# Attention scores as 24-row tiles of the array with one head per 32 rows; maxima split on GpSimd, second LayerNorm scaled on ScalarE

## The chip, the cores and the metric

The kernel runs on one core of one Trainium2 chip. The metric is the device time of an execution in microseconds (us). Engines: PE is TensorE, PEld its weight loads, DVE is VectorE, ACT is ScalarE, POOL is GpSimd, SP is SyncE, which here only issues transfers. The engines run on their own and wait for each other through semaphores.

## The reference, cut to what matters

The input is 32 sequences of 128 tokens with 128 channels (4096 tokens). Layer 0 is a modulated linear map with a clip and a mixture of 8 experts, 2 for each token. Layer 1 is an adapter, attention with 16 heads of 8 channels inside each sequence, and a second mixture of experts. The change touches this part:

```python
h = _layernorm(x, ln1_g, ln1_b)                      # 128 channels
q, k, v = jnp.split(h @ w_qkv + b_qkv, 3, axis=-1)   # each to (sequence, 128 tokens, 16 heads, 8)
scores = jnp.einsum('bqhd,bkhd->bhqk', q, k) / np.sqrt(8)
attn = jax.nn.softmax(scores, axis=-1)
o = jnp.einsum('bhqk,bkhd->bqhd', attn, v).reshape(B, S, D)
x = x + o @ w_o + b_o
h = _layernorm(x, ln2_g, ln2_b)                      # then gate, top 2 of 8, experts, weighted sum
```

## The kernel before, in words

The program is a chain of stages, each a block with its own instruction list for every engine, and a barrier between two: `setup` and `layer0`, `experts0`, `pre_attention`, `attention`, `experts1`, `finish`. In the profiled execution `pre_attention` runs from about 264 to 363 us, `attention` from 363 to about 650 us with its tail.

**pre_attention** goes over eight groups of four sequences. It blends the expert rows, runs the adapter and the first LayerNorm, and computes q and k transposed (channels on partitions, 512 tokens wide). Each is stored in two parts, a high one rounded to fp32r (`high_part`, ACT, L1078) and the rest (`lows`, DVE, L1030), so that products of parts keep fp32's precision. SP writes a group's four arrays to DRAM in one transfer (`store`, L961), and behind it on SP's queue stand the fetches for group n + 3 (L955, L860).

**attention** goes over 32 sequences s, in rounds; u = s mod 4. SP loads q and k for two sequences at a time: `load_pair` puts three parts one above the other on 96 partitions (q high, low, high; k high, high, low), so one matmul adds three products of parts. Four heads lie together on 32 rows, and a head is picked by masks: km holds k four times with all heads but one zeroed (`mask_k`, one of the four on POOL, L1426, three on ACT, L1553), qm holds the same for q, filled by 12 small transfers for each pair (L1410). Thus one matmul gives the scores of four heads as 128x512:

```python
nc.tensor.matmul(ps1[:, g % 2, :], qp[b][:, g, tok(u)], km[p][:, g]...)            # score, L1589
nc.tensor.matmul(ps2[:, g % 2, :]..., kp[b][:, g, tok(u)], qm[b][:, g, :, tok(u)]) # shift, L1596
nc.tensor.matmul(ps2[:, g % 2, :], selr[:, g, :], mxT[p][:])                       # shift, L1598
```

The order on PE is written out by hand. A round for s has four steps g = 0 to 3: the score of sequence s + 1 into one of two banks of ps1, then the shift of s into one of two banks of ps2. The shift computes the scores again, transposed (keys on partitions), and adds the negated maxima, which come transposed as mxT. Then follow: the output projection of s - 3 (L1634), `mix` of s - 1 (probabilities times values, L1616), `turn_max` (transposes of the maxima of s + 1, L1605), and `total` of s - 1 (sums, L1625). `mix` and `total` use four column tiles of 32.

DVE takes maxima over ps1 (L1473), four for each sequence; score g waits for maximum g - 2, since it uses the same bank. Then DVE splits the maxima into a high part and a rest (L1480, L1482), which `turn_max` waits for. It also divides (L1487, L1490) and adds the projection (L1495). ACT takes four exponentials of ps2 (L1565), masks k, and copies the transposed maxima (`copy_max`, L1545); the next round's first shift waits for this copy. POOL masks k, spreads the values into a block diagonal (`spread_v`, L1435), and sends rows.

Second LayerNorm and routing of a group of four sequences run inside the rounds, two groups behind, at fixed u: DVE takes variances in u = 3, POOL the reciprocal root in u = 1 (L1257), DVE normalises in u = 0 (L1272), PE transposes in u = 1 (L1281), computes gate logits in u = 2 (L1298) and ranks in u = 3 (L367). POOL scatters rows to DRAM with indirect transfers (L404), three in u = 1 and five in u = 2, and joins the streams (L1264). After the last round the same steps run for the last two groups one after another, with 8 scatters each.

## Time and profile before

| | us |
|---|---|
| median of 3 timed runs | 926.86 (926.55 to 927.62) |
| span of the profiled execution, first to last instruction | 835.4 |
| difference, around the span | 91.5 |
| PE busy in the span | 614.0 |
| DVE busy | 531.2 |
| ACT busy | 349.9 |
| POOL busy | 427.8 |

The profiled execution's own time isn't given beside its span; the median of the timed runs stands for it. The span is that of one execution, from the first instruction to the last. Busy time is the sum over an engine's instructions; where matmuls overlap they count once. A row of the timeline has a start, a duration, the engine, the line, the tile written and those read, their shapes and a count; in brackets stands the idle time before it and what ended it. A count over 1 means that a run of the same instructions was merged, and the duration is that of the whole run. An fp32 matmul leaves two records, an fp32r matmul one.

### The profile page before, as it was taken

How to read it: one execution, taken by the hardware profiler on the slowest of the kernel's cores; microseconds unless marked ns; L12 is line 12 of the kernel's file. 1: busy time of each engine (PE TensorE's matmuls, PEld its weight loads, DVE VectorE, ACT ScalarE, POOL GpSimd, SP SyncE). 2: the span in 40 equal slices, each digit the busy share in tenths (PEclk: the TensorE clock that was granted, in tenths of full speed). 3: DMA queues.
4: the chain of work that ended last, by engine and by line, in shares of the span. 5: the costliest groups of instructions: out<-in, count | busy, mean ns of one | idle time of the engine just before them, and what ended most of it. 6: DMA issues, size and time to landing. Idle time of an engine off the chain costs nothing. (4 is left out here: it accounts for less than half of the span.)

```text
span 835.4 us, 19142 instructions
## 1 busy us (share of the span) xinstructions
PE 614.0 (73%) x5686; PEld 501.2 (60%) x5686; DVE 531.2 (64%) x1601; ACT 349.9 (42%) x673; POOL 427.8 (51%) x528
## 2 busy tenths in 40 slices
PE   1799932999990675629999988999740599999920
PEld 0466622989980443416777666667530499999910
DVE  1455542767761789854788688789543377777708
ACT  0433411555440232326777676767410244334300
POOL 1177760767765454361444675676573055555530
PEclk9999985999995599966999999999955699999975
DMA  7711153777753254733444344356115788888318
GB/s 233 150 52 52 51 98 96 222 200 206 212 154 84 58 164 154 207 101 61 90 97 105 93 100 105 77 127 124 29 42 76 252 273 248 245 247 250 104 61 266
DMA packets 98617, 116.28 MB, mean 139 GB/s; under 512 B 16225, under 2 KB 78209, under 8 KB 98433
## 3 DMA queue, kind: packets, MB, share of 16 engines
q1 hardware_dynamic: 78784, 92.38, 41.9%
q0 software_dynamic: 9216, 18.96, 7.2%
q10 hardware_dynamic: 10560, 4.24, 2.5%
q8 instruction: 29, 0.48, 0.2%
q14 instruction: 28, 0.22, 0.1%
HBM read 81.84 MB, written 33.69 MB: 138 GB/s over the span
## 5 line engine op out<-in xcount | busy, mean ns | idle before, releaser
L404 POOL DMA_INDIRECT dispatch_rows<-row,index x128 | 128.2, 1002 | 96.2 <-DVE index L385 61.1
L740 POOL DMA_INDIRECT expert_rows<-fo,to x80 | 78.4, 980 | 84.8 <-DVE fo L1773 70.3
L1473 DVE TENSOR_REDUCE mneg<-ps 128x4 f32<-128x512 f32 x128 | 86.8, 690 | 41.7 <-PE ps L1589 39.5
L740 POOL DMA_INDIRECT expert_rows<-eo,to x80 | 77.1, 964 | 56.2 <-ACT eo L831 31.1
L1565 ACT ACTIVATE prob<-ps 128x512 f32<-128x512 f32 x128 | 76.3, 598 | 53.4 <-PE ps L1598 48.0
L713 DVE CAST xh<-psT 128x256 fp32r<-128x256 f32 x80 | 34.0, 425 | 97.1 <-PE psT L683 97.1
L1763 PE MATMUL psO<-wb,fh 128*128 128x128 f32 x640 | 77.8, 275 | 0.0
L731 PE MATMUL psA<-xh,wh 128*128 128x256 f32 (+1 forms) x240 | 75.4, 314 | 0.0
L1589 PE MATMUL ps<-km,qp 96*128 96x512 f32 x128 | 58.5, 460 | 23.0 <-POOL km L1426 17.4
L1763 PEld LDWEIGHTS psO<-wb,fh 128*128 128x128 f32 x640 | 74.9, 192 | 0.0
L731 PE MATMUL psA<-xh,wl 128*128 128x256 f32 (+1 forms) x240 | 68.7, 286 | 0.0
L731 PE MATMUL psA<-xl,wh 128*128 128x256 f32 (+1 forms) x240 | 68.4, 285 | 0.0
L1809 ACT ACTIVATE fh<-psA,wb 128x256 f32<-128x256 f32 x80 | 33.6, 471 | 80.2 <-PE psA L731 80.2
L1426 POOL TENSOR_SCALAR km<-kp,const 96x512 fp32r<-96x512 f32 x32 | 52.6, 1644 | 23.7 <-DMA kp<-qk_parts 18.8
L1553 ACT ACTIVATE km<-kp,const 96x512 fp32r<-96x512 f32 x96 | 61.9, 711 | 6.8 <-PEq L950 5.5
L1596 PE MATMUL ps<-qm,kp 96*128 96x512 f32 x128 | 55.4, 433 | 0.7 <-ACT mxT L1545 0.4
L1598 PE MATMUL ps<-mxT,selr 128*128 128x512 f32 x128 | 53.2, 416 | 0.0
L1589 PEld LDWEIGHTS ps<-km,qp 96*128 96x128 f32 x128 | 25.8, 203 | 41.1 <-issue 25.9
L731 PEld LDWEIGHTS psA<-xh,wh 128*128 128x128 f32 (+1 forms) x240 | 44.1, 184 | 0.0
L731 PEld LDWEIGHTS psA<-xl,wh 128*128 128x128 f32 (+1 forms) x240 | 44.0, 183 | 0.0
L1435 POOL COPY vb<-V 128x32 f32 (+1 forms) x128 | 21.1, 209 | 44.4 <-PE psAO L1625 44.4
L731 PEld LDWEIGHTS psA<-xh,wl 128*128 128x128 f32 (+1 forms) x240 | 43.7, 182 | 0.0
(203 smaller groups left out, 1504.1 us busy)
## 6 DMA issues: line engine op xcount, KB each, us to landing
wb<-in_W1b SPq DMA_DIRECT2D x40, 578.0 KB
w<-in_W SPq DMA_DIRECT2D x40, 304.0 KB
qk_parts<-qk SPq DMA_DIRECT2D x8, 1024.0 KB, 4.9
qp<-qk_parts SPq DMA_DIRECT2D x48, 128.0 KB, 3.1
kp<-qk_parts SPq DMA_DIRECT2D x48, 128.0 KB, 3.7
qm<-qk_parts SPq DMA_DIRECT2D x192, 32.0 KB
xs<-dispatch_rows SPq DMA_DIRECT2D x40, 129.0 KB
xt<-dispatch_rows SPq DMA_DIRECT2D x40, 129.0 KB
```

The lines of the kernel that those rows point to most:

```text
L404: pool.indirect_dma_start(out=m.xbuf, out_offset=bass.IndirectOffsetOnAxis(ap=r.index[b][:, c:c + 1], axis=0), in_=r.row[b][:, c // TOPK, ...
L713: v.tensor_copy(z.xh[q][:], z.psT[:, q, 0:SLOTS]).then_inc(z.x_high, 1)
L731: ins = z.m.nc.tensor.matmul(out, w[k][q][:, columns], x[k][q][:], start=(k == 0), stop=(k == 2), skip_group_check=True)
L740: pool.indirect_dma_start(out=m.ybuf, out_offset=bass.IndirectOffsetOnAxis(ap=to[b][:, a:a + 1], axis=0), in_=out[b][:, a, :], in_offset=N ...
L1426: ins = nc.gpsimd.tensor_scalar(km[p][:, :, j, :], kp[b][:, :, tok(u)].bitcast(F32), mask(j), None, ALU.mult)
L1473: ins = nc.vector.tensor_reduce(mneg[p][:, g, :], ps1[:, g % 2, :].rearrange("p (j k) -> p j k", j=4), AX_X, ALU.max, negate=True)
L1553: ins = nc.scalar.activation(km[p][:, :, j, :], kp[b][:, :, tok(u)].bitcast(F32), ACT.Copy, scale=mask(j))
L1565: nc.scalar.activation(prob[p][:, g, :], ps2[:, g % 2, :], ACT.Exp, scale=ATT_SCALE).then_inc(exped, 1)
L1589: nc.tensor.matmul(ps1[:, g % 2, :], qp[b][:, g, tok(u)], km[p][:, g].rearrange("p j k -> p (j k)"), start=True, stop=True).then_inc(score ...
L1596: nc.tensor.matmul(ps2[:, g % 2, :].rearrange("p (j k) -> p j k", j=4), kp[b][:, g, tok(u)], qm[b][:, g, :, tok(u)], start=True, stop=False)
L1598: nc.tensor.matmul(ps2[:, g % 2, :], selr[:, g, :], mxT[p][:], start=False, stop=True).then_inc(shifted, 1)
L1763: ins = nc.tensor.matmul(psO[:, q, a * P:(a + 1) * P], h[q][:, k, a * P:(a + 1) * P], wb[b][:, WIDE + k * P:WIDE + (k + 1) * P], start=(k ...
```

## The change

q and k are laid out anew: head 4g + j has 32 rows of partitions (32g to 32g + 31) and its own place j in the free dimension; 24 of the rows are used, three parts of 8 channels. The weights of q and k are reordered once on ACT so that the projection gives this order. Three arrays each of q and k are stored now (the doubled high part is written by ACT with one activation of twice the width), in four transfers a group, and a pair is loaded in eight transfers. Masks, km and qm are gone. A score is now four matmuls with 24 rows and 128 columns, on rows 32g and up; the shift of group (g + 2) mod 4 stands between them, on other rows. Splitting the maxima moves to POOL (`part_max`). Normalising moves from DVE to ACT, with an offset (minus mean times root) from DVE. The root moves from u = 1 to u = 0, and scatters are spread as 3, 3 and 2 over u = 0, 1 and 2.

```diff
+    m.wqk, m.qkb = m.sb("wqk", [P, 2 * P]), m.sb("qkb", [P, 2])
...
-def load_pair(m, sp, n, b):
-
-    for side, parts in ((m.qp[b], (0, 1, 0)), (m.kp[b], (2, 2, 3))):
-        for r, a in enumerate(parts):
-            sp.dma_start(side[32 * r:32 * r + 32].bitcast(F32),
-                         m.qk_dram[a, :, bass.ds(n * PAIR, PAIR)].rearrange("(g r) t -> r g t", g=HG)
-                         ).then_inc(m.pair_in[b], 16)
+def load_pair(m, sp, i, b):
+
+    half = slice(b * PAIR, (b + 1) * PAIR)
+    for g in range(HG):
+        for side, at in ((m.qp[b], 0), (m.kp[b], SPLIT)):
+            source = m.qk_dram[bass.ds(i, 1), g, at:at + SPLIT, :, half].rearrange(
+                "a s (d j) t -> (a s d) j t", j=HG)
+            sp.dma_start(side[32 * g:32 * g + HROWS].bitcast(F32), source).then_inc(m.pair_in[b], 16)
+
+
+PAIR_LOADS = 16 * 2 * HG
...
+                    for g in range(HG):
+                        sp.dma_start(m.qk_dram[bass.ds(n, 1), g].rearrange("a c p t -> (a p) c t"),
+                                     qk[b][32 * g:32 * g + 32].bitcast(F32)).then_inc(qk_out[b], 16)
...
+                    both = qk[b][:, 0:3:2, :] if w == 0 else qk[b][:, 3:5, :]
+                    nc.scalar.activation(both, bc(psQK[:, w, :].unsqueeze(1), P, 2, GW), ACT.Identity,
+                                         bias=m.qkb[:, w:w + 1]).then_inc(high, 1)
+
+                act.wait_ge(m.late_ld, LATE_LOADS)
+                nc.scalar.activation(m.wqk[:].rearrange("p (g d j) -> p g d j", d=DK, j=HG),
+                                     m.wqkv[:, 0:2 * P].rearrange("p (g j d) -> p g d j", j=HG, d=DK),
+                                     ACT.Copy).then_inc(ordered, 1)
...
-def post_normalise(q, dve, n):
+def post_centre(q, dve, n):
 
     dve.wait_ge(q.rooted, n + 1)
-    wait(dve, q.turned, n)
+    wait(dve, q.normed, n)
+    q.m.nc.vector.scalar_tensor_tensor(out=q.offset[:], in0=q.mv[:, :, 0], scalar=-1.0, in1=q.rstd[:],
+                                       op0=ALU.mult, op1=ALU.mult).then_inc(q.centred, 1)
+
+
+def post_normalise(q, act, n):
+
+    act.wait_ge(q.centred, n + 1)
+    wait(act, q.turned, n)
     for t in range(GT):
-        ins = q.m.nc.vector.tensor_scalar(q.norm[:, t, :], post_stream(q, n, t), q.mv[:, t, 0:1],
-                                             q.rstd[:, t:t + 1], ALU.subtract, ALU.mult)
+        ins = q.m.nc.scalar.activation(q.norm[:, t, :], post_stream(q, n, t), ACT.Identity,
+                                       bias=q.offset[:, t:t + 1], scale=q.rstd[:, t:t + 1])
     ins.then_inc(q.normed, 1)
...
-                    hold(m, sp, shifted, 8 * (n - 1))
-                    hold(m, sp, km_pool, 2 * (n - 1))
-                    hold(m, sp, km_act, 2 * (n - 1))
                     if not isinstance(n, int):
-                        load_pair(m, sp, n, b)
-                    if isinstance(n, int):
-                        sp.wait_ge(zeroed[b], 1)
-                    for j in range(4):
-                        for r, a in enumerate((0, 1, 0)):
-                            rows = slice(32 * r + 8 * j, 32 * r + 8 * j + 8)
-                            source = m.qk_dram[a, :, bass.ds(n * PAIR, PAIR)].rearrange("(g j r) t -> j r g t", g=HG, j=4)[j]
-                            sp.dma_start(qm[b][rows, :, j, :].bitcast(F32), source).then_inc(qm_in[b], 16)
+                        hold(m, sp, shifted, 8 * (n - 1))
+                        load_pair(m, sp, i, b)
                 table_sync(tiles, sp)
 
             @block.gpsimd
...
-                def mask_k(s, u, i):
-                    p, b = u % 2, u // 2
-                    if p == 0:
-                        pool.wait_ge(pair_in[b], 96 * (i + 1))
-                    hold(m, pool, scored, 4 * (s - 1))
-                    for j in range(KM_POOL):
-                        ins = nc.gpsimd.tensor_scalar(km[p][:, :, j, :], kp[b][:, :, tok(u)].bitcast(F32), mask(j), None,
-                                                      ALU.mult)
-                    ins.then_inc(km_pool, 1)
+
+                def part_max(s, p):
+                    pool.wait_ge(maxed, 4 * s + 4)
+                    hold(m, pool, turned, s - 1)
+                    x = xm[p][:]
+                    hi, lo = (bass.AP(x.tensor, x.offset + w, [list(x.ap[0]), [32, HG], [P, 4]]) for w in range(2))
+                    nc.gpsimd.tensor_copy(hi.bitcast(F32R), mneg[p][:]).then_inc(link, 1)
+                    hold(m, pool, link, s + 1)
+                    nc.gpsimd.tensor_tensor(lo, mneg[p][:], hi, ALU.subtract).then_inc(parted, 1)
 
...
-                parts = {1: range(0, 3), 2: range(3, 8)}
-                for s, u, i in rounds(pool, SEQS, GT, head=3 * GT):
-                    mask_k(s, u, i)
+                part_max(0, 0)
+                parts = {0: range(0, 3), 1: range(3, 6), 2: range(6, 8)}
+                for s, u, i in rounds(pool, SEQS, GT, head=3 * GT, tail=GT):
+                    if not is_last(s, SEQS):
+                        part_max(s + 1, (u + 1) % 2)
+                    if u == 0 and due(i - 2):
+                        post_root(post, pool, i - 2)
+                    spread_v(s, u % 2)
                     if u in parts and due(i - 3):
                         post_scatter(post, pool, i - 3, 0, parts[u])
-                    if u == 1 and due(i - 2):
-                        post_root(post, pool, i - 2)
-                    if not first(s):
-                        spread_v(s - 1, (u - 1) % 2)
-                    if is_last(s, 2):
-                        nc.gpsimd.memset(qm[1][:].bitcast(F32), 0.0).then_inc(zeroed[1], 1)
                     if u == 3 and due(i - 2):
                         post_join(post, pool, i - 2)
-                spread_v(SEQS - 1, 1)
...
+                    wait(dve, parted, s - 1)
...
-                    dve.wait_ge(maxed, 4 * s + 4)
-                    wait(dve, turned, s - 1)
-                    x = xm[p][:]
-                    hi, lo = (bass.AP(x.tensor, x.offset + w, [list(x.ap[0]), [32, 4], [130, 4]]) for w in range(2))
-                    nc.vector.tensor_copy(hi.bitcast(F32R), mneg[p][:]).then_inc(link, 1)
-                    dve.wait_ge(link, s + 1)
-                    nc.vector.tensor_tensor(lo, mneg[p][:], hi, ALU.subtract).then_inc(parted, 1)
...
+                    if u == 0 and due(i - 2):
+                        post_normalise(post, act, i - 2)
...
-                def score(s, u, i, g):
-
-                    p, b = u % 2, u // 2
-                    wait(pe, maxed, 4 * s + g - 1)
-                    nc.tensor.matmul(ps1[:, g % 2, :], qp[b][:, g, tok(u)], km[p][:, g].rearrange("p j k -> p (j k)"),
-                                     start=True, stop=True).then_inc(scored, 1)
-
-                def shift(s, u, g):
-
-                    p, b = u % 2, u // 2
-                    wait(pe, exped, 4 * s + g - 1)
-                    nc.tensor.matmul(ps2[:, g % 2, :].rearrange("p (j k) -> p j k", j=4), kp[b][:, g, tok(u)], qm[b][:, g, :, tok(u)],
-                                     start=True, stop=False)
-                    nc.tensor.matmul(ps2[:, g % 2, :], selr[:, g, :], mxT[p][:], start=False, stop=True
-                                     ).then_inc(shifted, 1)
+                def score(s, u, g, j):
+
+                    head = slice(32 * g, 32 * g + HROWS)
+                    return nc.tensor.matmul(ps1[:, g % 2, j * P:(j + 1) * P], qp[u // 2][head, j, tok(u)],
+                                            kp[u // 2][head, j, tok(u)], start=True, stop=True, skip_group_check=True)
+
+                def shift(s, u, g, bank, j):
+
+                    head = slice(32 * g, 32 * g + HROWS)
+                    return nc.tensor.matmul(ps2[:, bank, j * P:(j + 1) * P], kp[u // 2][head, j, tok(u)],
+                                            qp[u // 2][head, j, tok(u)], start=False, stop=(j == 3),
+                                            skip_group_check=True)
+
+                def lower(s, u, g, bank):
+
+                    rows = slice(32 * g, 32 * g + 32)
+                    nc.tensor.matmul(ps2[:, bank, :], selr[rows, :], mxT[u % 2][rows, :], start=True, stop=False,
+                                     skip_group_check=True)
 
...
                     for g in range(HG):
                         if more:
-                            score(*nxt, g)
+                            wait(pe, maxed, 4 * (s + 1) + g - 1)
                         if g == 0:
-                            if u % 2 == 0:
-                                pe.wait_ge(qm_in[u // 2], 16 * 12 * (i + 1))
                             pe.wait_ge(mxT_done, s + 1)
-                        shift(s, u, g)
+                        wait(pe, exped, 4 * s + g - 1)
+                        if more:
+                            score(s + 1, nxt[1], g, 0)
+                        lower(s, u, opposite(g), g % 2)
+                        for j in range(4):
+                            if more and j < 3:
+                                ins = score(s + 1, nxt[1], g, j + 1)
+                                if j == 2:
+                                    ins.then_inc(scored, 1)
+                            ins = shift(s, u, opposite(g), g % 2, j)
+                        ins.then_inc(shifted, 1)
                     if u == 1 and due(i - 2):
                         post_turn(post, pe, i - 2)
```

## Rows read from the trace of the kernel before

**Rows 1.** The page, part 1: busy time, share of the span, instructions of each engine.

```profile
PE 614.0 (73%) x5686; PEld 501.2 (60%) x5686; DVE 531.2 (64%) x1601; ACT 349.9 (42%) x673; POOL 427.8 (51%) x528
```

**Rows 2.** Stretches of attention: us, busy time by engine (count), PEclk, DMA share, GB/s.

```profile
377.00:390.00 13.00, 11.24 (x27) 8.11 (x27) 5.50 (x10) 7.79 (x13) 1.56 (x1) 0.50 0.13 20
...
430.00:590.00 160.00, 146.58 (x1944) 109.89 (x1942) 128.10 (x379) 114.88 (x199) 102.44 (x166) 0.99 0.46 103
```

**Rows 3.** Timeline of DVE: maxima of seven of the sequences.

```profile
400.05 2.95 DVE L1473 TENSOR_REDUCE mneg<-ps 128x4 f32<-128x512 f32 x4 [1.90 <-PE ps L1589]
...
429.82 2.79 DVE L1473 TENSOR_REDUCE mneg<-ps 128x4 f32<-128x512 f32 x4
...
509.81 2.67 DVE L1473 TENSOR_REDUCE mneg<-ps 128x4 f32<-128x512 f32 x4
...
517.67 2.67 DVE L1473 TENSOR_REDUCE mneg<-ps 128x4 f32<-128x512 f32 x4 [0.33 <-PE ps L1589]
...
524.17 2.66 DVE L1473 TENSOR_REDUCE mneg<-ps 128x4 f32<-128x512 f32 x4
...
531.11 2.81 DVE L1473 TENSOR_REDUCE mneg<-ps 128x4 f32<-128x512 f32 x4 [2.46 <-PE ps L1589]
...
538.66 2.68 DVE L1473 TENSOR_REDUCE mneg<-ps 128x4 f32<-128x512 f32 x4
```

**Rows 4.** Timeline of PE, one head group: start, us, engine, line, tiles, count.

```profile
511.36 0.39 PE L1589 MATMUL ps<-km,qp 96*128 96x512 f32 x1
511.59 0.40 PE L1596 MATMUL ps<-qm,kp 96*128 96x512 f32 x1
```

**Rows 5.** Timeline of PE, 519.6 to 523.3 us: the rest of a round.

```profile
520.23 1.08 PE L1616 MATMUL psAO<-prob,vb 128*32 128x128 f32 x32
521.61 0.66 PE L1605 MATMUL psM<-const,xmx 128*128 128x128 f32 x4 [0.30 <-DVE xmx L1482]
...
523.21 0.50 PE L1589 MATMUL ps<-km,qp 96*128 96x512 f32 x1
```

**Rows 6.** Waits of 377 to 600 us: waiting <- releaser: total us, times, longest.

```profile
PE ps L1589 <- POOL km L1426: 5.9, 5, 1.8
```

**Rows 7.** Timeline of PE elsewhere: 128 columns in fp32, 256 in fp32r.

```profile
300.91 1.06 PE L1117 MATMUL psD<-x1T,wd 128*32 128x128 f32 x8
...
721.80 0.28 PE L731 MATMUL psA<-xh,wl 128*128 128x256 f32 x1
721.92 0.28 PE L731 MATMUL psA<-xh,wh 128*128 128x256 f32 x1
```

**Rows 8.** Groups by line, POOL, 377 to 600 us: busy us, mean ns | idle before.

```profile
L404 POOL DMA_INDIRECT dispatch_rows<-row,index x41 | 40.7, 994 | 32.3 <-DVE index L385 22.2 <-issue 8.2 <-PE ps L1589 1.2
L1435 POOL COPY vb<-V 128x32 f32 (+1 forms) x120 | 19.8, 209 | 44.4 <-PE psAO L1625 44.4
L1257 POOL TENSOR_TENSOR rstd<-var,minus_half 128x4 f32<-128x4 f32 x6 | 6.4, 1060 | 4.5 <-DVE var L1250 4.4
```

**Rows 9.** Timeline: four 128x128 with scale and bias on ACT, four normalised on DVE.

```profile
35.20 1.50 ACT L590 ACTIVATE y<-psY,vec,dcoef 128x128 f32<-128x128 f32 x4
...
604.09 1.28 DVE L1272 TENSOR_SCALAR norm<-X,mv,rstd 128x128 f32<-128x128 f32 x4 [2.20 <-POOL rstd L1257]
```

**Rows 10.** Timeline, start of the attention stage.

```profile
369.00 1.19 PE L1589 MATMUL ps<-km,qp 96*128 96x512 f32 x2 [11.50 <-POOL km L1426]
...
376.42 0.60 ACT L1545 ACTIVATE mxT<-psM 128x512 fp32r<-128x512 f32 x1 [9.82 <-PE psM L1605]
...
377.16 0.77 PE L1596 MATMUL ps<-qm,kp 96*128 96x512 f32 x1 [0.35 <-ACT mxT L1545]
```

**Rows 11.** The page, part 6: DMA issues, KB each, median us to landing.

```profile
qk_parts<-qk SPq DMA_DIRECT2D x8, 1024.0 KB, 4.9
```

**Rows 12.** Timeline of SPq, a store and what follows it.

```profile
297.19 0.39 SPq L961 DMA_DIRECT2D qk_parts<-qk  x1
...
298.17 1.02 SPq L860 DMA_DIRECT2D gr<-expert_rows  x1
```

110 lines of the change are left out of this document (50 added, 60 removed).

## The prediction, made before the changed kernel was timed

> **What bounds the kernel now.** I read the page's busy shares first. Over the whole span TensorE leads with 73% and VectorE has 64% [rows 1], but that mixes all stages and decides nothing. All edits sit in attention and in the stage ahead of it, so the second view is the table of stretches. Between 430 and 590 us TensorE is busy for 146.6 of 160 us at full clock, VectorE for 128.1, ScalarE for 114.9, GpSimd for 102.4 [rows 2]: TensorE is the engine to follow there, and VectorE is close behind. Third, the maxima on the timeline of VectorE, four reductions for each sequence, mark the rounds. Early rounds, in which no second LayerNorm or routing is due, are (429.82 - 400.05)/5 = 5.95 us long. With that work a set of four (u = 3, 0, 1, 2) takes 7.86 + 6.50 + 6.94 + 7.55 = 28.85 us [rows 3]. The stretch from 430 to 590 holds 22 rounds, 7.2 us each, the same.
>
> Inside a round, four steps (one for a group of four heads) come first. On TensorE a step is three matmuls of 512 columns, 0.23 us apart [rows 4], so 0.69 us; VectorE's four reductions take 2.67 us, 0.67 each [rows 3]. So the steps are paced by two engines at once, and a faster TensorE alone gains next to nothing in them. The rest, from the mixing matmuls to the next score, takes 523.21 - 520.23 = 2.98 us, of which 0.30 is a wait for the split maxima: 2.7 us of work [rows 5]. What isn't work in the rounds is mostly a wait for the masked keys: 5.9 us in 5 waits for GpSimd [rows 6], and the 2.46 us for which VectorE stands at 531.11 [rows 3] are its echo.
>
> **The step after the change.** Three loads and three matmuls become nine of each: four scores and four shifts of 24 rows by 128 columns, and one 32-row matmul of 512 columns. Scores use one row group, the other five the opposite one. No row shows an array split by rows. The nearest rows: 32 records of matmuls into four column tiles (L1616) take 1.08 us [rows 5], 8 records of the same 128 fp32 columns without tiles (L1117) take 1.06 [rows 7]. So four tiles really run side by side, loads included. For loads of 128 columns, the fp32r pairs at L731 stand 0.12 us apart [rows 7], so a load costs 0.12 at most. For matmuls: 512 fp32r columns cost 0.23, 256 cost 0.12; I take 0.06 for 128. If the two row groups run side by side and a load hides behind its own group's matmuls, the longer side is the 512 columns, the first shift, and three more shifts paced by loads: 0.23 + 0.06 + 3 x 0.12 = 0.65 us. That is below VectorE's 0.67, so VectorE paces the steps.
>
> A plain round, from its first score at 0: the last score lies behind three loads, reduction 0 starts at 0.7 (three loads 0.36, one matmul 0.06, about 0.17 until a result is out, that is 0.39 of record less 0.23 of spacing in rows 4, and the handover), reductions end at 1.37, 2.04, 2.71 and 3.38. Step 3 waits for reduction 1, starts at 2.1 and ends at 2.75; projection 0.3; then 2.7 us: 5.8 us against 5.95.
>
> One rule speaks against the edit. The Trainium skill (TensorE: Matmul & The Clock Gate, section LDWEIGHTS) says that a load costs its columns and not its rows. By it the 24-row loads are no cheaper than the 96-row ones, there are three times as many, and side by side is all that saves the step; the sum above prices them in full already, so it stays.
>
> **Maxima on GpSimd.** Cast and subtraction leave VectorE (about 0.4 us in a round) and become two GpSimd instructions of 128x16. GpSimd's copy of 128x32 takes 0.21 us, its power of 128x4 takes 1.06 [rows 8]. I take 0.21, since these are a copy and a subtraction: with three handovers 0.6 us, so the transposes may start at 3.38 + 0.6 = 4.0. TensorE gets there at 2.75 + 0.3 + 1.0 = 4.05: hidden. At 1.06 each they'd be ready at 5.7 and cost 1.6 us a round, 50 us in 31 rounds; a gain isn't possible beyond VectorE's 0.4. Queued behind them on GpSimd: the root (1.06), the spread values (4 x 0.21 in record, 0.65 in fact) and two or three scatters, each 0.99 plus 0.3 of issue [rows 8]. In a round u = 0 that is 1.06 + 0.65 + 3.9 = 5.6 us, and the next maxima come 5.8 us or more after the last: it fits with little to spare. The masked key (1.6 us a round of GpSimd, 1.9 of ScalarE) is gone, and the 12 small loads for each pair with it.
>
> **Normalise on ScalarE.** It must come in round u = 0 between the exponentials and the copy of the next maxima, which the next round's first score now waits for. The chain: reductions end at 3.4 (as in a plain round), GpSimd splits until 4.0, root until 5.1, VectorE's offset until 5.4, four activations of 128x128 take 1.50 us (the same form at L590) [rows 9] until 6.9, copy of the maxima 0.6 until 7.5. TensorE alone would need 5.8: a new stall of 1.7 us. Round u = 0 goes from 6.50 to 7.5. Round u = 1 is the plain 5.8 and four transposes, 0.5 (between rows 5's 0.66 for four of the same form and their spacing): 6.3 against 6.94. Round u = 2 has four fp32 matmuls of 136 columns, two records each, each record a little over the 0.13 of 128 columns [rows 7], so 1.15: 6.95 against 7.55. In round u = 3 VectorE is last: 7.86 less the 0.4 that moved, and the late start less 0.3: 7.15. Sum 27.9 against 28.85, or 0.95 for four rounds; for 22 rounds -5 us. The five early rounds go from 5.95 to 5.8, -0.8.
>
> **The start.** In attention's first 27 us TensorE has a granted clock of 0.50 [rows 2], the row from 377 to 390, which is 1.2 GHz, after it stood idle. The stage opens at 362.8, but the first score runs at 369.00, having waited 11.5 us, last for GpSimd's masked key, and the first shift at 377.16 [rows 10]. After: scores at once, at half clock 16 loads of 0.24 each (twice the 0.12), 3.8 us, then 0.9 until the last reduction ends, 0.6 for GpSimd, 1.1 for transposes at half clock, 0.6 for the copy: first shift 7.0 us into the stage, at 369.8 instead of 377.2. I take -7. From 377.16 to the maxima at 400.05 there are three rounds in 22.9 us [rows 3, 10]. After: two at half clock with steps of 1.3, 4 x 1.3 + 2.6 = 7.8 each, and one of 5.9: 21.5, -1.4.
>
> **What is added ahead.** The store of q and k grows from 1024 KB, landing in 4.9 us [rows 11], to 1536 KB in four issues of 0.39 each [rows 12]. The last one is waited for by the whole stage: 1.2 us of issues and about 0.4 for ScalarE's doubled write of k: +1.7. The other seven have the fetch at L860 behind them on SP's queue. Its issue stands there for 1.02 us anyway [rows 12], since it waits for its buffer, so 0.8 us of the 1.2 are covered; with more traffic beside it I book +1 in all, 0 to +7 as bounds. ScalarE's doubled writes of groups 0 to 6 lie in its idle time. At the end, twice, normalising takes 1.50 and an offset of 0.2 instead of 1.28 on VectorE [rows 9], and this chain is serial: +1.
>
> **Sum.** -7 - 1.4 - 0.8 - 5 + 1.7 + 1 + 1 = -10.5 us. The profiled execution has a span of 835.4 us; the three timed runs have a median of 926.86, so 91.5 us lie around the span, and nothing in them changes. 926.9 - 10.5 = 916 us. On its own this case ranges from 904 to 926.
>
> **Rivals.**
> 1. Loads don't run side by side. Then nine loads at 0.12 make a step of 1.08 us: step 3 ends at 4.3, not 2.75, +1.55 a round, 31 rounds, less about 2 where VectorE is last in u = 3: +46, so 962 us, slower than before. Against it are the column tiles, whose 32 loads fit into 1.08 us [rows 5]; for it, that none of these is a row tile. It decides from a step of 0.77 us on: 4 x 0.77 - 2.75 = 0.33 us, which in 31 rounds is the whole gain.
> 2. A load waits for its own group's matmul. Step: 0.23 + 4 x (0.12 + 0.06) = 0.95 us, +1.05 a round, +31: 947 us. The unsplit array doesn't do that: its 512-column matmuls stand at 0.23 with a load each [rows 4]. The Trainium skill has this rule (same page, Part 3, The mechanism: a load overlaps a running matmul only when the row group differs); the trace disagrees for the whole array and shows no row tile.
> 3. 128 columns of fp32r cost what fp32 costs. An fp32 matmul of 128 columns is two records, 8 in 1.06 us [rows 7], so 0.22 to 0.26 each. No row has fp32r below 256 columns. Step 0.23 + 4 x 0.22 = 1.11: +1.7 a round, +50: 966; with the row groups one after another too, 1.99 a step, (1.99 - 0.65) x 4 x 31 = 166 and less the same 2 more: 1080.
> 4. GpSimd comes late. If scatters and root don't fit between two maxima, the split waits about 0.6 us in 18 rounds: +11, and the time is 927, no change.
>
> **Chances.** Forecast 0.54, of which 0.02 shows too little to be told from no change; rival 1 0.12, rival 2 0.06, rival 3 0.15, rival 4 0.08; 0.05 for a gain beyond 904, if shorter waits also keep the clock up. Within 0.2% (1.9 us, what a measurement of this kernel can tell) fall the 0.02 and 0.05 of rival 4. Slower: 0.33 and 0.02 of rival 4, 0.35. Faster: 0.58. The range that leaves out under 2 in 10 goes from 900 to 968, over most of rivals 1 to 3.
>
> **What would show it.** In the changed profile: first maxima of a round 0.67 us apart each (a step over 0.8 on TensorE is rival 1, 2 or 3: the spacing of shifts tells which, 0.12 mine, 0.18 the second, 0.22 the third); no wait for a masked key; first shift about 7 us after the stage opens; ScalarE's copy of maxima last in u = 0, rounds of 7.5 us there and 5.8 in the early ones; transposes of maxima that wait for GpSimd under 0.2 us. I am wrong if early rounds are over 5.95 us.

## The result: 8 to 9 per cent slower

Changed kernel 1006.39 us (median of 4, 1001.98 to 1017.28), kernel before 927.24 beside it; ratio 1.083, 95% interval 1.078 to 1.088. The forecast was 916, its range 900 to 968. It was wrong, in sign too.

On the chip of that comparison the kernel before takes 94 us more and the changed one 99 us more than on the chips of most later runs. In the changed kernel's profile there, engines wait for something that the trace can't name, also in stages that the change doesn't touch (waiting <- releaser: us in total, times, longest):

```profile
ACT fh L1814 <- remote: 49.7, 11, 4.7
DVE xh L715 <- remote: 45.1, 15, 3.4
ACT s L607 <- remote: 24.7, 5, 7.7
ACT mxT L1548 <- remote: 24.6, 4, 6.2
```

A later run of the same kernel on another chip (e1_after) has no such wait and takes 907.33 us against 833.58 for the kernel before: ratio 1.090, 1.086 to 1.094. The loss is the same in kind, and traces are compared there: span 900.9 against 834.2 (e0_before). The page of e1_after, busy time and PEclk in 40 slices (compare [rows 1]):

```profile
span 900.9 us, 20237 instructions
PE 650.8 (72%) x6454; PEld 550.9 (61%) x6454; DVE 497.8 (55%) x1509; ACT 310.1 (34%) x610; POOL 383.0 (43%) x559
PEclk9999967999955788658888696867866589999975
```

VectorE, ScalarE and GpSimd have less to do than before, TensorE 38 us more (613.0 in e0_before): its clock is below full in most slices of the attention. Cut into stages (start to end; us; busy time and count by engine; PEclk; DMA share; GB/s), with cuts at the first and last exponential, the kernel before:

```profile
272.00:377.70 105.70, 61.96 (x300) 40.53 (x301) 81.55 (x214) 33.90 (x57) 48.45 (x57) 0.82 0.47 137
377.70:597.90 220.20, 203.88 (x2645) 152.46 (x2648) 167.50 (x478) 158.29 (x273) 117.74 (x201) 0.97 0.43 94
597.90:834.20 236.30, 153.82 (x1384) 150.21 (x1376) 142.67 (x447) 60.57 (x130) 105.35 (x108) 0.81 0.63 183
```

and the changed one:

```profile
272.00:388.80 116.80, 70.77 (x325) 48.27 (x325) 73.01 (x207) 37.31 (x52) 37.10 (x47) 0.72 0.60 154
388.80:665.70 276.90, 233.44 (x3386) 195.42 (x3388) 143.35 (x398) 111.10 (x207) 85.97 (x242) 0.77 0.19 54
665.70:900.90 235.20, 153.55 (x1388) 149.78 (x1380) 140.88 (x442) 63.77 (x137) 105.87 (x108) 0.82 0.63 184
```

Up to 272 us they are alike. The loss is 11.1 us up to the first exponential and 56.7 in the rounds; the tail gains 1.1.

**The start.** SyncE's queue in e1_after, one group (start, us, then line, transfer, count):

```profile
304.81 3.43 SPq L968 DMA_DIRECT2D qk_parts<-qk  x4
308.28 1.54 SPq L961 DMA_DIRECT2D gbu<-cond_rows  x1
309.87 1.82 SPq L862 DMA_DIRECT2D gr<-expert_rows  x1
```

One store issue took 0.39 us before [rows 12]; the four take 3.4, and the fetches behind them are slow too. The last three groups' twelve store issues and the waits between them end at 375.2, and the first score runs at 380.23 (its row and that of the first shift below):

```profile
354.69 20.46 SPq L968 DMA_DIRECT2D qk_parts<-qk  x12
...
380.23 1.12 PE L1580 MATMUL ps<-kp,qp 24*128 24x128 f32 x8 [11.98 <-PEq L956]
387.21 0.79 PE L1593 MATMUL ps<-mxT,selr 32*128 32x512 f32 x1
```

**The rounds.** In round u = 2 of a steady group three engines stand still in turn. TensorE, ScalarE and GpSimd of e1_after:

```profile
573.58 1.08 PE L1611 MATMUL psAO<-prob,vb 128*32 128x128 f32 x32
579.44 0.80 PE L1629 MATMUL psW<-wo,oT 128*128 128x128 f32 x2 [4.78 <-ACT row L395]
...
572.08 1.09 ACT L1556 ACTIVATE prob<-ps 128x512 f32<-128x512 f32 x2 [0.58 <-PE ps L1586]
578.73 0.38 ACT L395 ACTIVATE row<-psW 128x256 f32<-128x256 f32 x1 [5.56 <-DMA dispatch_rows<-row,index]
...
573.35 0.21 POOL L1441 CAST xmx<-mneg 128x16 fp32r<-128x16 f32 x1 [1.10 <-DVE mneg L1486]
573.94 0.65 POOL L1450 COPY vb<-V 128x32 f32 x4
575.11 1.01 POOL L406 DMA_INDIRECT dispatch_rows<-row,index  x1 [0.52 <-issue]
576.43 0.96 POOL L406 DMA_INDIRECT dispatch_rows<-row,index  x1 [0.30 <-issue]
```

Read backwards: TensorE's projection waits for ScalarE's copy of rows (L395), since both use psW. ScalarE may not overwrite its row buffer until the last of the eight scatters of the group before has landed. The last two now stand on GpSimd's queue behind the maxima of the next round and spread_v. Five such rounds take 13.2 to 14.1 us; the same rounds before took 6.7 to 8.7.

The table gives what each run's trace has in the 31 round lengths between first exponentials: their sum, the time in them at a granted clock of 0.50 (1.2 GHz, not 2.4), and, for sequences 12 to 27, the median length by u of the rounds that ran wholly at full clock ("-" where none did). Medians are in us, "before" is the kernel before on the same chip. e8_lower_rows took 897.5 and 898.9 us in two executions and 915.2 and 916.5 in two slow ones, and the table has the middle of the first two.

```
run               median  before  31 rounds  at 0.50  u0    u1    u2     u3
e0_before         832.8   833.6   217.7      15       6.9   7.5   7.2    7.3
e1_after          907.3   833.6   273.5      123      -     6.4   -      -
e2_norm_dve       896.3   833.6   271.1      131      6.3   6.4   -      -
e3b_split_dve     885.3   831.5   258.8      131      -     -     8.2    -
e4_scatter_early  881.5   831.5   252.5      117      -     -     7.2    -
e6_one_store      893.4   831.5   279.9      146      -     6.4   -      -
e7_all_four       857.3   831.5   242.3      101      6.2   6.4   7.2    -
e8_lower_rows     898.2   834.3   281.8      97       7.4   7.8   8.6    -
e9_fill_128       856.3   834.3   244.9      26       7.1   7.5   8.3    8.6
e10_fill_24       861.8   834.3   253.6      104      -     6.7   7.5    -
e11_rows_128      986.2   834.3   378.1      212      -     -     10.0   -
e12_fill_cheap    848.5   833.3   232.9      66       -     6.4   -      7.4
e13_fill_two      846.3   833.3   231.0      61       6.2   6.4   -      7.4
e14_after_fill    937.5   833.3   304.8      96       8.9   7.5   -      8.1
e15b_fill_gaps    841.3   833.3   226.5      42       6.1   6.4   7.7    7.5
e16_fill_three    845.9   832.6   228.1      33       6.5   6.8   7.6    7.9
```

### The profile page after: what moved, and what is told of

Same layout as the page of the kernel before. It is cut to its first block and busy times, and to the rows that moved or that the text cites. A ratio compares the mean times of both kernels' runs of the same rounds, so it can differ in the third digit from the quotient of the medians.

```text
span 1000.2 us, 20237 instructions
## 1 busy us (share of the span) xinstructions
PE 695.5 (70%) x6454; PEld 576.0 (58%) x6454; DVE 490.1 (49%) x1509; ACT 308.2 (31%) x610; POOL 386.0 (39%) x559
## 5 line engine op out<-in xcount | busy, mean ns | idle before, releaser
L1486 DVE TENSOR_REDUCE mneg<-ps 128x4 f32<-128x512 f32 x128 | 82.8, 687 | 116.7 <-PE ps L1580 113.4
L1580 PE MATMUL ps<-kp,qp 24*128 24x128 f32 x512 | 82.2, 328 | 35.9 <-PEq L956 12.7
L1580 PEld LDWEIGHTS ps<-kp,qp 24*128 24x128 f32 x512 | 72.7, 230 | 48.5 <-issue 28.8
L1441 POOL CAST xmx<-mneg 128x16 fp32r<-128x16 f32 x32 | 6.8, 212 | 194.1 <-DVE mneg L1486 194.1
L1586 PEld LDWEIGHTS ps<-qp,kp 24*128 24x128 f32 x512 | 79.4, 235 | 0.2
L1586 PE MATMUL ps<-qp,kp 24*128 24x128 f32 x512 | 75.5, 301 | 0.0
L1593 PE MATMUL ps<-mxT,selr 32*128 32x512 f32 x128 | 68.8, 596 | 0.1
L1611 PE MATMUL psAO<-prob,vb 128*32 128x128 f32 x1024 | 56.4, 388 | 0.6 <-issue 0.6
L1620 PE MATMUL psAO<-prob,const 128*32 128x128 f32 x1024 | 46.3, 319 | 11.1 <-issue 11.1
L809 PE MATMUL psO<-w,eh 88*128 88x128 f32 x320 | 45.8, 290 | 4.5 <-DVE eh L823 4.5
```

The lines of the kernel that those rows point to most:

```text
L809: ins = nc.tensor.matmul(psO[:, q, a * P:(a + 1) * P], h[q][:, k, a * P:(a + 1) * P], w[b][0:HALF, 4 * HALF + k * P:4 * HALF + (k + 1) * P ...
L1486: ins = nc.vector.tensor_reduce(mneg[p][:, g, :], ps1[:, g % 2, :].rearrange("p (j k) -> p j k", j=4), AX_X, ALU.max, negate=True)
L1580: return nc.tensor.matmul(ps1[:, g % 2, j * P:(j + 1) * P], qp[u // 2][head, j, tok(u)], kp[u // 2][head, j, tok(u)], start=True, stop=Tru ...
L1586: return nc.tensor.matmul(ps2[:, bank, j * P:(j + 1) * P], kp[u // 2][head, j, tok(u)], qp[u // 2][head, j, tok(u)], start=False, stop=(j ...
L1593: nc.tensor.matmul(ps2[:, bank, :], selr[rows, :], mxT[u % 2][rows, :], start=True, stop=False, skip_group_check=True)
L1611: nc.tensor.matmul(psO[32 * g:32 * g + 32, p, 0:P], vb[p][:, 4 * g + j, :], prob[p][:, g, j * P:(j + 1) * P], start=(j == 0), stop=(j == 3 ...
```

## The experiments

**e0_before and e1_after**: the two kernels again, three rounds on one chip. 

> The kernel before, unchanged. Theory A (the profile of 835.4 us of span is not an execution like the timed ones, 926.9 us): its span here is about 925 us, and the 91.5 us that I laid around the span lie inside it, as stalls that the first profile doesn't show, in stages that the change doesn't touch too. Theory B (the time around the span is real): span 835, time 927.

> The changed kernel, unchanged. Theory A: time 1002 to 1007 us, span 2 us less, as in its first profile; the difference in span to the kernel before on the same chip is about 77 us, and most of it lies in the attention stage. Theory B: 77 us of difference in time and 165 in span.

Measured: above. Less than one part in a hundred of the ratio hangs on the chip.

**e2_norm_dve**: the second LayerNorm is normalised on VectorE again.

```diff
-    ins = q.m.nc.scalar.activation(q.norm[:, t, :], ..., bias=q.offset[:, t:t + 1], scale=q.rstd[:, t:t + 1])
+    ins = q.m.nc.vector.tensor_scalar(q.norm[:, t, :], ..., q.mv[:, t, 0:1], q.rstd[:, t:t + 1], ...)
```

> The changed kernel with the second LayerNorm normalised on VectorE again, everything else as changed. Theory 1 (the new chain through ScalarE before the copy of the maxima stalls rounds u = 0 by 1.5 us): 6 to 10 us faster than the changed kernel. Rival (the time goes into a lower clock of TensorE and into engines that stand still together): within 3 us of it.

896.3 against 907.3: 11 us; theory 1, a little above its range. At full clock a round u = 0 takes 7.95 us in e1_after (two rounds, of sequences 8 and 28) and 6.1 to 6.4 here, so the serial chain over ScalarE costs 1.6 to 1.9 us, about the 1.7 of the forecast.

**e3b_split_dve**: the maxima are split on VectorE, behind its reductions.

```diff
-                nc.gpsimd.tensor_copy(hi.bitcast(F32R), mneg[p][:])...; nc.gpsimd.tensor_tensor(lo, ...)
+                nc.vector.tensor_copy(hi.bitcast(F32R), mneg[p][:])...; nc.vector.tensor_tensor(lo, ...)
```

> The changed kernel with the split of the maxima back on VectorE (the two instructions directly behind its four reductions), all else as changed. Theory 1 (the scatters of u2 hold ScalarE): the scatters of u2 still stand behind spread_v, which waits for the mix before it, but no longer behind the maxima of the next round; the wait for dispatch_rows shrinks from 5.5 to 2 to 4.5 us a group and the chain to the transposes is about 0.5 us shorter a round: 890 to 903 us. Rival, the GpSimd split itself is what lengthens every round (its two instructions start 0.3 to 1.5 us late): 28 rounds shorter by 0.8 or more, under 885 us. Rival 2, VectorE is the bound, as the prediction had it, and 0.5 us more work on it a round costs as much: 910 to 925 us.

885.3, between the ranges of the first two. The wait for dispatch_rows is 4.8 us in all where e1_after has 27.3 (see e4): freed from the maxima, GpSimd's queue reaches its scatters sooner. So most of this gain is the stall's and not the split's own 0.4 us. VectorE is not the bound (rival 2 falls). The run doesn't part the two effects; that most of it is the stall is argued from the waits and from e4.

**e4_scatter_early**:

```diff
-                parts = {0: range(0, 3), 1: range(3, 6), 2: range(6, 8)}
+                parts = {0: range(0, 4), 1: range(4, 8)}
-                    spread_v(s, u % 2)
                     if u in parts and due(i - 3):
                         post_scatter(post, pool, i - 3, 0, parts[u])
+                    spread_v(s, u % 2)
```

> The changed kernel, but GpSimd's eight scatters of a group go out in rounds u0 and u1 (four each) and ahead of spread_v, instead of three, three and two in u0, u1 and u2 behind it. Theory 1: in e1_after ScalarE stood still in each steady u2 round until the last two scatters had landed (its row copy waited for dispatch_rows 27.3 us in 5 places, 5.6 at most), with PE and DVE behind it (u2 rounds 13 to 14 us against 7.2 before), and part of the granted clock fell after these gaps. Then the wait goes to under 1 us each, u2 rounds come to 7 to 8.5 us, the half clock inside the attention (123 us in e1) falls below 90 us, and the kernel takes 862 to 882 us. Rival 1, the clock falls because the 24-row work leaves too little for TensorE to do: the wait goes but the half clock stays over 110 us, 878 to 890 us. Rival 2, the wait is covered by another that ends at the same time: over 898 us.

881.5, which lies in the range of theory 1 and of rival 1; the half clock decides between them. ScalarE's waits ahead of its row copy in the rounds, e1_after and then e4_scatter_early:

```profile
ACT row L395 <- DMA dispatch_rows<-row,index: 27.3, 5, 5.6
ACT row L395 <- DVE logits L338: 0.8, 1, 0.8
```

```profile
ACT row L395 <- DVE logits L338: 7.2, 6, 1.9
```

The wait is gone and 26 us with it, but the time at half clock fell only from 123 to 117. Steady u2 rounds are 7.2 to 8.6 us long, as theory 1 had it. Rival 1 was right on the clock: without the stall it still falls, elsewhere (more on this at e14_after_fill).

**e6_one_store**: rows of q and k in the order 16 d + head, so that one transfer stores all 128 rows. The bias comes in one load too.

```diff
-                    for g in range(HG):
-                        sp.dma_start(m.qk_dram[bass.ds(n, 1), g].rearrange("a c p t -> (a p) c t"),
-                                     qk[b][32 * g:32 * g + 32]...)
+                    sp.dma_start(m.qk_dram[bass.ds(n, 1)].rearrange("a c p t -> (a p) c t"), qk[b][:]...)
```

> The changed kernel with the rows of q and k in another order (row 16d + head instead of 32 group + 4d + head), so that a group's six parts go out in one transfer from 128 rows instead of four from 32 rows each, and the bias in one load; the attention's loads read the same bytes and stay 16 of 96 KB a group. Theory 1, the four issues of 3.4 to 4.2 us each on SyncE's queue hold the loads queued behind them: the last psV matmul comes 9 to 12 us sooner (368.0 in e1_after, 356.6 before) and the attention opens 4 to 6 us sooner after it; 888 to 896 us. Rival, the half more bytes (1.5 MB a group instead of 1.0) cost that time whatever the form: within 4 us of e1_after's 907. Rival 2: the loads of the attention get slower from the new row order, and a part of the gain is lost there: 896 to 903 us.

893.4. The first exponential comes at 373.7 instead of 388.8, 15 us sooner and 4 sooner than in the kernel before, with the same bytes, as in theory 1. On SyncE's queue:

```profile
304.41 0.38 SPq L967 DMA_DIRECT2D qk_parts<-qk  x1
304.84 0.54 SPq L961 DMA_DIRECT2D gbu<-cond_rows  x1
305.42 1.40 SPq L862 DMA_DIRECT2D gr<-expert_rows  x1
```

So the form of the transfers cost 15 us, not their size. The loads changed with the store (last section): the 16 load issues ahead of the last stores stand from 336.9 to 350.2 in e1_after, 13.3 us, and from 327.6 to 336.6 here, 9.1 us. What each has of the 15 us was not separated. In this run more of the rounds ran at half clock (146), which took a part back.

**e7_all_four**: the four edits together; what is left is the tiles, with no masked keys. 

> The changed kernel with four parts altered at once: one store a group (as in e6_one_store), scatters in u0 and u1 (as in e4_scatter_early), split of the maxima on VectorE, second LayerNorm's normalisation on VectorE (as in e2_norm_dve). What is left of the change is one head per 32 rows, 24-row score tiles, no masked keys. Theory 1: the four costs add up (about -17, -30, -5, -11 of 907): 836 to 852 us, so the 24-row tiles with everything else put right are still not faster than before by more than a few us. Rival 1 (the granted clock falls from the narrow tiles themselves): 855 to 875 us with over 90 us at half clock inside the attention. Rival 2 (the parts were all of the loss and the tiles gain what was predicted): under 830 us.

857.3, rival 1's case: 50 us of the 74 are found, but the kernel is still 1.032 (1.029 to 1.036) of the one before. Where a round keeps full clock it is shorter than before in u1 (6.4 against 7.5), equal in u2, and in u0 6.2 against 6.9; that one is the round of sequence 12 alone, which took 6.3 before. In the stretch 430:590, TensorE is as busy as it was in [rows 2], and its granted clock 0.83 instead of 0.99:

```profile
430.00:590.00 160.00, 146.81 (x2308) 123.61 (x2307) 114.92 (x365) 68.52 (x124) 56.26 (x122) 0.83 0.28 66
```

**e8 to e11** ask why, all on e7_all_four.

```diff
+                def fill(s, u, count):                      # e9: rows = 0:128, e10: rows = 0:24
+                    for k in range(count):
+                        nc.tensor.matmul(psO[:, u % 2, 2 * P:3 * P], m.wo[rows, :], m.ident[rows, :], ...)
                     for g in range(HG):
+                        if g % 2 == 0:
+                            fill(s, u, 2 + g)
-                    nc.tensor.matmul(ps2[:, bank, :], selr[rows, :], mxT[u % 2][rows, :], ...)
+                    nc.tensor.matmul(ps2[:, bank, :], selr[:, g, :], mxT[u % 2][:], ...)      # e8
-                    head = slice(32 * g, 32 * g + HROWS)
+                    head = slice(0, P)                                                       # e11
```

> e7_all_four with extra matmuls whose result nobody reads (128 rows, 128 columns, float32, constants on both sides), two ahead of a round's first step and four ahead of its third, where TensorE waits 0.4 to 0.5 us for the exponentials. Nothing is left out. 192 of them, about 0.13 us each at full clock by the transposes' 0.60 us for four: 25 us of work, more than half of it in gaps. Theory R (rows in use): half clock in the rounds under 50 us, 840 to 855 us although work was added. Theory G (gaps): the same here, since the gaps are filled too; e10_fill_24 tells the two apart. If neither (the clock falls for something outside TensorE): half clock stays at 90 to 110 us and the time rises by 8 to 20 us, to 865 to 877.

> e9_fill_128 with the same extra matmuls over 24 rows instead of 128: the same places, columns and count. Theory R (rows in use): the clock is not better than in e7_all_four (90 to 115 us of the rounds at half), and the time is 862 to 877 us. Theory G (gaps): as e9_fill_128, under 50 us at half clock and 840 to 855 us.

The same stretch, e9_fill_128 and then e10_fill_24:

```profile
430.00:590.00 160.00, 155.72 (x2501) 133.11 (x2501) 111.22 (x353) 65.68 (x122) 57.02 (x122) 0.98 0.27 63
```

```profile
430.00:590.00 160.00, 156.50 (x2385) 134.36 (x2381) 104.69 (x324) 62.76 (x113) 54.64 (x120) 0.80 0.25 62
```

TensorE is busy alike in both. With 128 rows the clock is back at 0.98 (26 us at half in the rounds), with 24 rows it is 0.80 (104 us). This is the clearest pair of the study: between these two the granted clock went with the rows of the fill and not with gaps. Over whole executions, all four of e9 have a mean clock of 0.877 to 0.882, those of e10 0.835 to 0.847, of e7 0.828 to 0.831. The profiled execution of e10 is 867.9 us, over its median. The time of e9 is e7's (856.3): the fill costs what the clock returns. The median of e10 is 861.8, just under the range of theory R; two of its four executions took 855.0 and 857.0, as long as e9. The fill of 128 rows also makes full-clock rounds longer (by 0.9 to 1.1 us against e7, the one of 24 rows by 0.3), and the pair doesn't part rows from that.

> e7_all_four, with the maxima added (lower) over all 128 rows by a masked selr for each group of heads, as before the change, instead of over the group's own 32 rows: the same number of instructions and columns, the same result, more rows of the array in use in one instruction of nine of a step. In e7_all_four TensorE was as busy as before in a stretch of the attention (146.8 of 160 us against 146.1), and its granted clock was 0.83 against 0.99, 100.7 us of the rounds at half clock against 15.4. Theory R (the clock falls because so few rows are in use at a time): fewer than 75 us at half clock, 835 to 850 us. Theory G (the clock falls after gaps and stalls, whatever the rows): within 10 us of e7's 100.7 and within 4 us of its 857; slower by up to 6 if the full-row instruction can no longer run beside the tiles of another group.

Theory G has the half clock right (97 us), and both miss the time: 898.2, 41 us slower. The instructions that add the maxima start here, one a step, in e8_lower_rows:

```profile
466.98 0.49 PE L1588 MATMUL ps<-mxT,selr 128*128 128x512 f32 x1
468.11 0.49 PE L1588 MATMUL ps<-mxT,selr 128*128 128x512 f32 x1
469.12 0.49 PE L1588 MATMUL ps<-mxT,selr 128*128 128x512 f32 x1
```

and in e7_all_four:

```profile
456.55 0.49 PE L1586 MATMUL ps<-mxT,selr 32*128 32x512 f32 x1
456.89 0.49 PE L1586 MATMUL ps<-mxT,selr 32*128 32x512 f32 x1
458.28 0.50 PE L1586 MATMUL ps<-mxT,selr 32*128 32x512 f32 x1
458.77 0.49 PE L1586 MATMUL ps<-mxT,selr 32*128 32x512 f32 x1
```

Steps of tiles alone overlap in pairs, 0.34 and 0.49 us apart, and the four take 2.2 us from first start to last; with one full-array instruction in each they stand 1.0 to 1.1 us apart (3.2 for the four). A full-clock round grows by 1.2 us in u0 and 1.4 in u1 and u2, 0.3 to 0.35 us a step. The Trainium skill (TensorEngine Tiling (Array Packing), section Key Properties) says that a change of tiling mode drains TensorE; this trace agrees, but doesn't part a drain from the plain loss of running side by side. TensorE has hardly a gap left between 430 and 590 us (159.7 of 160 us busy), and its clock is 0.84 there: gaps in TensorE's work are not what holds it down in this run.

> e7_all_four with the score and shift matmuls over all 128 rows instead of the 24 of one head; it leaves out that heads are kept apart (each score is the sum over four heads), and zeroes the four tiles once during the stage before. Instructions, columns, waits and bytes are the same; tiles of different groups can no longer run at the same time. Theory R (rows in use): half clock in the rounds under 30 us, and full-clock rounds of 6.2 to 7.5 us: 825 to 850 us, although each instruction can do no more beside another. Theory G (gaps): half clock stays at 80 to 120 us and the time is 855 to 880 us.

986.2, 212 us at half clock. It doesn't test the clock as meant: with no tiles side by side TensorE is busy without a break, rounds are 10 to 14 us long, and the clock is low all the same:

```profile
430.00:590.00 160.00, 159.88 (x1472) 125.80 (x1460) 71.18 (x201) 43.82 (x75) 30.52 (x77) 0.73 0.18 42
```

So rows in use are not the whole rule: theory R, which expected under 30 us, fails here, as it did in e8. What sets the clock stays open: the fill of e9 is fp32 and stands by itself, the 128-row instructions of e8 and e11 are fp32r, and no run takes these apart (below, four fp32r matmuls in e12 help about as much as two fp32 ones in e13). What e11 shows is the worth of side by side: a steady round u2 at full clock takes 10.0 us and not 7.2, 2.9 us a round or 89 in 31 rounds by estimate; the rest of the 129 us goes along with the longer time at half clock.

**e12 to e16** put less fill into places where TensorE waits anyway.

```diff
-                        if g % 2 == 0:
-                            fill(s, u, 2 + g)
+                        if g == 2:
+                            fill(s, u, 2)          # e13; e12: 4 in float32r; e16: 1 at g = 0 as well
+                    if u > 1 and due(i - 2):
+                        fill(s, u + 1, 3)          # e15b, besides e13's: behind mix, ahead of the projection
```

> e7_all_four with four extra 128-row matmuls a round that nobody reads, ahead of the third step only, and in float32r (selr on both sides, one pass of 128 columns): about 0.11 us each at full clock, 0.45 us a round, the size of the gap in which TensorE waits there for the exponentials (0.43 to 0.49 us). In e9_fill_128 the fill took the half clock of the rounds from 100.7 to 25.6 us, but its own work (full-clock rounds 7.11, 7.5, 8.26, 8.6 us against 6.2, 6.4, 7.15, 6.8) gave it all back. If the clock follows the work on all rows, little of it is enough and it fits the gap: half clock 15 to 45 us, time 826 to 842. If it follows the amount (six float32 matmuls a round were needed): half clock 60 to 100 us, 845 to 860 us.

> e7_all_four with two float32 128-row matmuls ahead of a round's third step (about 0.19 us each by e9_fill_128's rounds, 0.4 us, a third of its fill). If a third of the fill is enough for the clock: half clock under 45 us, 828 to 842 us. If the clock's gain goes with the amount of fill: half clock 60 to 85 us, 842 to 856 us. Rival: any fill costs more than it returns: over 857.

848.5 us with 66 at half clock, 846.3 with 61: for both the second case of what was expected, in which the clock's gain goes with the amount of fill.

> e7_all_four with one float32 128-row matmul ahead of a round's first step and two ahead of its third: half of e9_fill_128's fill, spread over every round. By the amounts tried (none: 100.7 us at half clock and 857 us; two a round: 60.8 and 846; six: 25.6 and 856) 30 to 50 us at half clock and 838 to 848 us; if the clock has a step between two and six, under 20 us and 830 to 838 us.

845.9, as expected by the amounts: about half of e13's time at half clock, and the same time in all, since full-clock rounds grew by 0.3 to 0.4 us.

> e13_fill_two (two float32 128-row matmuls ahead of the third step) and three more in the steady u2 and u3 rounds behind the mix, where TensorE waits for VectorE or ScalarE before it projects (0.8 us five times in e7_all_four). In e13_fill_two the half clock was left in just these rounds (u2 8.6, u3 7.4, u0 8.4 us against 7.2, 6.8, 6.2 at full clock). If the clock is the rest of the loss: half clock from 60.8 to under 25 us, 825 to 838 us, level with the kernel before or faster. If the fill costs what it returns, as in e16_fill_three (32.5 us at half clock, 846 us, full-clock rounds 6.5, 6.8, 7.6, 7.9): 842 to 852 us.

841.3, between the two cases and just short of the second, ratio 1.0086 (1.0058 to 1.0114): the best version with tiles, still slower than before. Its half clock fell to 42 us, not under 25, against 15 before, so the clock may be the rest; but e16 had 33 us and was no faster, so the fill's own work may be it too. This stays open. e18_fill_every and e19_fill_u0, with a little more fill, ran on a chip where the kernel before took 932 us and rounds u0 of both were 14 to 16 us long; their 974.8 and 961.5 us decide nothing.

**e14_after_fill**: the changed kernel with e9's fill. 

> The changed kernel itself with e9_fill_128's fill (six float32 128-row matmuls a round), nothing else altered. It tells how much of the 57 us that its rounds lost goes through the clock while the stall of the u2 rounds, the four stores and the chain over ScalarE are still there. Theory (rows in use set the clock, the stall of u2 is apart): half clock in the rounds from 123 to under 60 us, u2 rounds still 12 to 14 us, and the time within 8 us of 907, since the fill costs what the clock gives back. Rival (the clock in the changed kernel falls after the gaps of 5 us in u2): half clock stays over 80 us and the time rises to 915 to 930 us.

937.5, nearer the rival, and over its range: the clock came back in part only (123 to 96, where e9 had 26), u2 rounds still took 14.1 to 15.8 us, and rounds at half clock followed them. A stall in u2 and the stretch behind it:

```profile
596.10:600.30 4.20, 0.00 (x0) 0.00 (x0) 0.41 (x2) 0.04 (x1) 2.01 (x3) 1.00 0.10 31
600.30:617.40 17.10, 16.42 (x170) 13.74 (x170) 7.95 (x37) 4.73 (x9) 2.30 (x7) 0.50 0.08 23
```

TensorE does nothing for 4.2 us, then its clock goes to 0.50 and stays there although it is busy again. The same happens in or right behind the other stalls of u2, and in half of the steady rounds u1, behind a wait of TensorE of 1.1 to 1.4 us at the end of u0. The fill costs 30 us net there. So the stalls have a share in the clock loss as well, which the narrow tiles hid in e4 (117 without it). The run differs from e9 in all four edits, so that share isn't split among them.

## Why the prediction was wrong

- **Shifts 0.12 us apart, tiles side by side, 128 columns of fp32r cheap**: right. Tiles of a group stand 0.11 us apart, two groups overlap, rivals 1 to 3 did not occur. But the round was not 5.8 us: at full clock early rounds are 6.1 (before: 5.9), which is over the 5.95 that the prediction named as its own sign of being wrong. Because two steps now run together, both banks turn over together: VectorE does two reductions in 1.29 us and waits 0.38, and TensorE waits 0.4 for the exponentials. Argued from the traces, not shown by a run. An early round of e1_after:

```profile
411.87 1.29 DVE L1486 TENSOR_REDUCE mneg<-ps 128x4 f32<-128x512 f32 x2 [3.07 <-PE ps L1580]
413.54 1.29 DVE L1486 TENSOR_REDUCE mneg<-ps 128x4 f32<-128x512 f32 x2 [0.38 <-PE ps L1580]
```

- **Rounds with the second LayerNorm**: close, where they kept full clock and met no stall. In e1_after those are 7.95 (u0), 6.4, 7.1 and 6.4 us (u2 and u3 from sequences 10 and 11, whose scatters are not yet due), 27.9 in all, and the sum had 27.9. That it fits to a tenth is luck: u0 was over its 7.5 and u3 under its 7.15.
- **The clock** was not a term of the sum beyond the first two rounds: 22 rounds were priced at full clock because they had it before [rows 2]. This step of the prediction failed, and it is the largest by the estimate below: the rounds of e1_after have 123 us at half clock, those of e0_before 15. In e7_all_four, eight early rounds at 6.1 and 23 steady ones at (6.2 + 6.4 + 7.2 + 7.4)/4 = 6.8 (u3 from e13) would be 205 us; they are 242. The estimate for the clock there is 37 us; e13 and e15b gave 11 and 16 back. Why the clock falls is open: 128-row fill brings it back (e9), more rows in the tiles' own instructions don't (e8, e11).
- **GpSimd**: "two or three scatters ... it fits with little to spare". Time on the queue was counted, and its fit was right, but not who waits for the last scatter. What had been a queue with slack got a new wait in front (the maxima), and ScalarE's buffer reuse behind it became a stall of 5.5 us a group: 26 us. Rival 4 named the late engine but priced another path, 11 us.
- **Normalise on ScalarE**: mechanism right, u0 as last chain; a stall of 1.7 us in each u0 forecast, 1.6 to 1.9 measured at full clock, 11 us in all by e2.
- **The start**: from stage opening to first shift 7.0 us, as forecast (380.2 to 387.2). The transfers failed: +1.7 and +1 in the sum, 15 measured by e6. An issue was priced at 0.39 from the row of a 128-row transfer; the four of 32 rows took 0.86 each in the group shown, and the median of all 32 is 1.40. The loads' issues, of which 16 lie ahead of the last stores (13.3 us; the 12 before took 6.8), weren't priced at all. With the one store of e6 the first exponential comes 4.0 us before that of e0_before, and the sum has -7 + 1.7 + 1 = -4.3.
- **The tail**: +1 forecast, -1.1 measured.
- **"91.5 us lie around the span"**: a wrong reading of two occasions. Where the kernel takes 833 us its span is 2 us less than its time, and where it takes 927 the changed kernel's span is within 2 us too. It moved no sign.

The parts, as medians: transfers 14, LayerNorm 11, scatters 26 (with the split 22 by another way), 50 for the four at once; of the 24 left in e7, 16 went with fill. The last 8 us are open. The runs lie on several chips, where the kernel before takes 831.5 to 834.3 us, so a part is known to some 3 us.

## What to carry to other kernels

When an instruction with a wait is put on an in-order queue, follow what stands behind it to whoever reuses a buffer only when that lands; slack on the queue is no cover for it. When work is cut into tiles of fewer rows, put a lower granted clock into the forecast as a case of its own, with rounds at both levels from rows. Price a transfer by a row of the same form (rows by parts), not of the same bytes.

## What the runs showed that was not expected

- With TensorE busy for 147 to 157 of 160 us, extra matmuls over 128 rows brought the granted clock from 0.83 to 0.98, over 24 rows not (0.80). Yet with 128 rows in every score and shift and TensorE busy for 159.9 of 160 us it was 0.73 (e11).
- One full-array instruction in a step of row tiles cost about 0.3 us a step (e8: 41 us over 128 steps).
- The same 96 KB load of 24 rows takes 0.78 us to issue in e1_after and 0.30 in e6_one_store, by the order of rows in DRAM alone (line, form, count: ns min/median/max):

```profile
L913 SPq DMA_DIRECT2D qp<-qk_parts x64: 780/783/892, 336.9 to 631.8; - x64
```

```profile
L913 SPq DMA_DIRECT2D qp<-qk_parts x64: 298/304/1372, 327.6 to 620.6; - x64
```
